# Down product of the third and fourth pair as seven block products for six of eight pieces, with the output projection last in the pair

## The reference

```python
# x: 8 chunks of 512 tokens, 512 features, float32
xn = layernorm(x)
q, k, v = xn @ Wq.T + bq, xn @ Wk.T + bk, xn @ Wv.T + bv
context = (elu(q) + 1) * cumsum((elu(k) + 1) * v, over tokens) * SCALE
s = context @ Wo.T + bo
h = fwht(xn * SU_ug) / 64                    # Walsh-Hadamard transform
u = silu(h @ W_gate.T * (Ws_gate * 64)) * (h @ W_up.T * (Ws_up * 64))   # 2048 wide
f = fwht(u * SU_dp) / 64 @ W_down.T * (Ws_down * 64)
out = x + s * silu(f)
```

## Time and profile before

| | |
|---|---|
| runs (3), us | median 1308.63, 1308.14 to 1309.26 |
| profiled execution, us | 1308.6 (the trace's span; no other run of it is shown) |
| granted TensorE clock | 0.998 of full |
| PE busy | 1276.1 us, 98%, 5968 matmuls |
| DVE busy | 886.8 us, 68% |
| ACT busy | 589.3 us, 45% |
| POOL busy | 59.1 us, 5% |
| DMA | 162 GB/s in the mean |

### The profile page before, as it was taken

One profiled execution on the slowest core, in us unless ns is written; L12 is line 12 of the kernel. 1 busy time (PEld: TensorE's weight loads), 2 busy tenths in 40 slices (PEclk: granted clock), 3 DMA queues, 4 the chain that ended last, 5 costly groups with the idle time before them and its releaser, 6 DMA issues.

```text
span 1308.6 us, 16031 instructions
## 1 busy us (share of the span) xinstructions
PE 1276.1 (98%) x5968; PEld 578.5 (44%) x5968; DVE 886.8 (68%) x1367; ACT 589.3 (45%) x880; POOL 59.1 (5%) x101
## 2 busy tenths in 40 slices
PE   5999999999999999999999999999999999999998
PEld 3544444444444444444444444444444444444443
DVE  6989999977756777777664755566762774555721
ACT  5875566631235655552324554442333654443220
POOL 1000101212000000110000000010000000000000
PEclk9999999999999999999999999999999999999999
DMA  9512552668764456653554323334453323323340
GB/s 374 212 65 89 174 188 113 216 243 286 207 251 149 145 207 239 206 185 129 193 193 161 129 97 129 112 147 161 161 195 129 126 99 127 119 107 112 114 156 37
DMA packets 56957, 212.03 MB, mean 162 GB/s; under 512 B 12208, under 2 KB 14512, under 8 KB 40368
## 3 DMA queue, kind: packets, MB, share of 16 engines
q1 hardware_dynamic: 45872, 179.55, 38.2%
q0 software_dynamic: 7536, 25.70, 5.8%
q10 hardware_dynamic: 3472, 5.77, 1.3%
HBM read 164.83 MB, written 46.16 MB: 161 GB/s over the span
## 4 chain that ended last, share of the span: by engine, by line
PE 58%; DVE 2%; issue 2%; ACT 2%; DMA 1%; DVEq 0%; ACTq 0%
PE bank L1875 39%; PE bank L1998 19%; DMA h_all<-scr_f 1%; DVE work L1261 1%; ACT work L922 1%; DVE work L1277 1%; ACT work L925 1%; DVE work L1267 0%; DVE h_all L1311 0%; DVE work L1302 0%; ACT work L905 0%; ACT L922 0%; DVE h_all L1424 0%; DVE h_all L1425 0%; DVE h_all L1601 0%
## 5 line engine op out<-in xcount | busy, mean ns | idle before, releaser
L1875 PE MATMUL bank<-xops,ring 128*128 128x512 f16 x2772 | 602.6, 379 | 8.6 <-DVE work L1261 3.3
L1875 PEld LDWEIGHTS bank<-xops,ring 128*128 128x128 f16 x2772 | 269.5, 98 | 340.6 <-issue 10.2
L1998 PE MATMUL bank<-h_all,ring 128*128 128x512 f16 x1536 | 333.8, 379 | 1.8 <-DMA ring<-scr_d 1.4
L1261 DVE TENSOR_TENSOR work<-bank,work 128x512 f32<-128x512 f32 x198 | 133.5, 686 | 163.2 <-PE bank L1875 150.5
L1998 PEld LDWEIGHTS bank<-h_all,ring 128*128 128x128 f16 x1536 | 149.9, 98 | 184.1 <-DVE work L1261 1.9
L1763 PE MATMUL bank<-xops,ring 128*128 128x512 f16 x1008 | 226.2, 381 | 2.5 <-DVE ring L1405 2.5
L905 ACT ACTIVATE work<-bank 128x512 f32<-128x512 f32 x198 | 117.8, 595 | 231.0 <-PE bank L1875 231.0
L1763 PEld LDWEIGHTS bank<-xops,ring 128*128 128x128 f16 x1008 | 98.4, 98 | 126.6 <-issue 10.5
L947 ACT ACTIVATE h_all<-work 128x512 f16<-128x512 f32 x128 | 78.1, 624 | 72.0 <-DVE work L1302 69.3
L1311 DVE TENSOR_TENSOR h_all<-work,h_all 128x512 f16<-128x512 f32 x128 | 87.4, 685 | 8.6 <-ACT h_all L947 7.5
L1267 DVE SCALAR_TENSOR_TENSOR work<-work 128x512 f32<-128x512 f32 x64 | 44.1, 689 | 49.7 <-ACT work L925 49.4
(11 more groups left out here) (210 smaller groups left out, 1023.0 us busy)
## 6 DMA issues: line engine op xcount, KB each, us to landing
ring<-scr_g SPq DMA_DIRECT2D x72, 1024.0 KB, 4.9
ring<-scr_d SPq DMA_DIRECT2D x32, 1024.0 KB, 5.4
scr_g<-ring SPq DMA_DIRECT2D x22, 512.0 KB, 3.3
h_all<-in_ug_t SPq DMA_DIRECT2D x8, 1024.0 KB, 12.3
x_res<-in_x_t SPq DMA_DIRECT2D x32, 256.0 KB, 4.3
out<-x_res SPq DMA_DIRECT2D x32, 256.0 KB, 4.4
scr_g<-ring POOLq DMA_DIRECT2D x12, 512.0 KB, 4.0
work<-in_x_t SPq DMA_DIRECT2D x6, 1024.0 KB, 7.3
```

The lines of the kernel that those rows point to most:

```text
L1261: dve.tensor_tensor(tile(g, j), at[:, :], tile(g, j), ALU.add).then_inc(summed, 1)
L1875: mm = pe.matmul(to[:, :], weight_of(slot, s, b, kk), at, start=(a == 0 and m in (P1, P2, P5)), stop=(a == 5), skip_group_check=True)
L1998: mm = pe.matmul(d_bank(c, t)[:, :], w[:, t, ws, :], at[:, s, :], start=(a == 0 and b == 0 and n == 0), stop=(a == KB - 1 and b == KB - 1 ...
```

## The change

Pairs 2 and 3 alone are changed in their products; what they need is prepared in pairs 0 and 1.

- The down product of both chunks of a pair is done at once. For pieces 0 to 5 it is seven block products of 18 matmuls, per output tile pair d = 0, 1 (`seven`); pieces 6 and 7 are added plainly (`rest`, 12 matmuls for each of four results and each d). That is 7 x 2 x 18 + 8 x 12 = 348 matmuls a pair, 384 before. It comes before the two Wo groups, which are now the last of the pair. The ring has four slots in these pairs.
- The operand sums of the hidden states are made as each up group ends: `hidden_sums` (four DVE operations of 128x512), `hidden_sums_high` (two on ACT), `hidden_sums_low` (two on DVE), in place of one high and one low operation.
- The S sums of the down weights are made in six units u = 0 to 5. ACT's queue stores the float32 down weights to memory (`df_stored`); POOL loads a unit (4 DMAs of 128 KB) and stores it (2 DMAs); DVE adds (`unit_add`, four operations of 128x256) and makes the low part (`unit_low`); ACT makes the high part (`unit_high`). Units 0 to 3 lie in the last chunk of pair 1, units 4 and 5 at the ends of groups 0 and 1 of pair 2.
- The down weights get one common scale, so squares of all four tiles are taken first: tiles 2 and 3 are loaded as a probe, 0 and 1 after them, then 2 and 3 again. The levels of the Hadamard butterfly on the down weights (`fly_down_level`) come one tile later in the order of the first groups, and the scale is worked out once, not four times.
- The statistics of pair 3 are taken in groups 8 and 10.
- Outputs of a pair are made together (`pair_outputs`): four around the Wo groups, four in groups 0 and 1 of the next pair (two each), and for the last pair after everything else.

```diff
+SEVEN_FROM, SEVEN = 2, 6
+REST = FP - SEVEN
+REST_BANKS = (6, 7)
+R11, R21, R22, R12 = range(7, 11)
+DOWN_SLOTS = (P1, P2, P6, P7, P5, R11, P4, P3)
+DOWN_ORDER = [(d, m) for ms in ((P1, P2), (P6,), (P7,), (P5,), (R11,), (R21,), (R22,), (R12,), (P4,), (P3,))
+              for d in range(2) for m in ms]
+DOWN_COPIES = ((0, P1), (1, P1), (0, P6), (1, P6), (0, P7), (1, P7))
+DOWN_SUMS = [(d, a) for a in ("22a", "11", "22", "12") for d in range(2)]
...
+PROBE, SQUARE_DOWN_AT = (2, 3, 0, 1), (15, 16, 19, 20)
...
-FLY_DOWN_AT, SCALE_DOWN_AT = (0, 1, 2, 3), 4
+FLY_DOWN_AT, SCALE_DOWN_AT = (1, 2, 3, 4), 4
...
+STATS_AT, LATER_STATS_AT = (16, 18), (8, 10)
...
+            load_probe(2)
+            load_probe(3)
...
                     store_piece(n)
+                if n == QKV_GROUPS - 1:
+                    load_down(0)
+                    load_down(1)
...
+            def load_unit(u):
+
+                d, q = u % 2, u // 2
+                if u < 2:
+                    pool.wait_ge(quad_done, 3 * KB)
+                    pool.wait_ge(df_stored, 16 * KB)
+                else:
+                    pool.wait_ge(unit_summed, u - 1)
+                for r in range(2):
+                    src = scr_df[d + 2 * r, :, :].rearrange("p (c k n) -> p c k n", c=2, k=FP)
+                    for half in range(2):
+                        pool.dma_start(unit_raw(u)[:, half, :, r, :], src[:, half, 2 * q:2 * q + 2, :]) \
+                            .then_inc(unit_loaded[u % 2], 16)
+
+            def store_unit(u):
+                d, q = u % 2, u // 2
+                pool.wait_ge(unit_made, u + 1)
+                to = scr_s[:, :, d, 512 * q:512 * q + 512].rearrange("o p n -> p o n")
+                for a in range(2):
+                    pool.dma_start(to[:, 2 * a:2 * a + 2, :],
+                                   unit_part(u, 2)[:, a, :].rearrange("p (o n) -> p o n", o=2)).then_inc(unit_stored[u % 2], 16)
...
+                if p == SEVEN_FROM - 1:
+                    load_unit(0)
+                    load_unit(1)
+                    for u in range(UNITS):
+                        store_unit(u)
+                        if u + 2 < UNITS:
...
+            def unit_high(u):
+                act.wait_ge(unit_summed, u + 1)
+                if u >= 2:
+                    act.wait_ge(unit_stored[u % 2], 32 * (u // 2))
+                act.activation(unit_out(u)[:, :, :, HI, :], unit_sums(u).rearrange("p c (m n) -> p c m n", m=4),
+                               ACT.Copy).then_inc(unit_hi, 1)
...
+            def hidden_sums_high(p, i):
+
+                g = QKV_GROUPS + 2 * i + 1
+                act.wait_ge(hidden_summed, sums_of_hidden(p, i))
+                act.activation(h[:, i, TILE_OF[C12], HI, :], tile(g, C12), ACT.Copy).then_inc(h_hi, 1)
...
+                three = work[:, 4 * (g % 3):4 * (g % 3) + 3, :]
+                act.activation(home(i)[:, :, HI, :], three, ACT.Copy).then_inc(hidden_sums_hi, 1)
...
                 if g:
                     take(p, g - 1, C12)
                 take(p, g, C11)
+                if p == SEVEN_FROM and g < UNITS - 4:
+                    unit_high(4 + g)
...
+            def seven_and_o(p):
+
+                seven_copy(p, 0, P1)
+                seven_copy(p, 1, P1)
+                seven_copy(p, 0, P6)
+                ctx_high(p, 0)
+                seven_copy(p, 1, P6)
+                seven_copy(p, 0, P7)
+                seven_copy(p, 1, P7)
+                ctx_high(p, 1)
+                if p < PAIRS - 1:
+                    x_high(p + 1, 0)
+                    t_high(p + 1, 0)
+                    x_high(p + 1, 1)
+                    t_high(p + 1, 1)
+                for d, j in GATE_ORDER:
+                    seven_gate(p, d, j)
+                o_groups(p)
...
-                if p < PAIRS - 1:
-                    x_high(p + 1, 0)
-                    t_high(p + 1, 0)
-                    x_high(p + 1, 1)
-                    t_high(p + 1, 1)
+                x_high(p + 1, 0)
+                t_high(p + 1, 0)
+                unit_high(0)
+                x_high(p + 1, 1)
+                unit_high(1)
...
+            def hidden_sums(p, i, part):
+
+                g = QKV_GROUPS + 2 * i + 1
+                b11, b22, b21, b12 = (tile(g, j) for j in (C11, C22, C21, C12))
+                if part == 0:
+                    dve.wait_ge(h_made, 32 * p + 4 * i + 4)
+                    prep.after(dve.tensor_tensor(b12, b12, b11, ALU.subtract))
+                    prep.after(dve.tensor_tensor(b22, b22, b12, ALU.subtract))
+                else:
+                    dve.tensor_tensor(b11, b22, b11, ALU.subtract)
+                    dve.tensor_tensor(b21, b21, b22, ALU.subtract).then_inc(hidden_summed, 1)
...
+            def hidden_sums_low(p, i):
+                g = QKV_GROUPS + 2 * i + 1
+                at = h[:, i, TILE_OF[C12], :, :]
+                dve.wait_ge(h_hi, 32 * p + 4 * i + 4)
+                dve.tensor_tensor(at[:, LO, :], tile(g, C12), at[:, HI, :], ALU.subtract).then_inc(h_ready, 1)
+                three = work[:, 4 * (g % 3):4 * (g % 3) + 3, :]
+                dve.wait_ge(hidden_sums_hi, sums_of_hidden(p, i))
+                dve.tensor_tensor(home(i)[:, :, LO, :], three, home(i)[:, :, HI, :], ALU.subtract) \
+                    .then_inc(hidden_sums_ready, 1)
...
+            def pair_outputs(p, ns):
+                for n in ns:
+                    d, j = OUT_ORDER[n]
+                    gated(2 * p + CHUNK_OF[j], d + 2 * ROW_OF[j])
...
+            def unit_add(u):
+
+                a11, a12, a21, a22 = (unit_raw(u)[:, half, :, r, :] for r in range(2) for half in range(2))
+                dve.wait_ge(unit_loaded[u % 2], 64 * (u // 2 + 1))
+                if u >= 2:
+                    dve.wait_ge(unit_made, u - 1)
+                prep.after(dve.tensor_tensor(unit_sum(u, S1), a21, a22, ALU.add))
+                dve.tensor_tensor(unit_sum(u, S3), a11, a21, ALU.subtract)
+                prep.after(dve.tensor_tensor(unit_sum(u, S2), unit_sum(u, S1), a11, ALU.subtract))
+                dve.tensor_tensor(unit_sum(u, S4), a12, unit_sum(u, S2), ALU.subtract).then_inc(unit_summed, 1)
...
+            def unit_low(u):
+                dve.wait_ge(unit_hi, u + 1)
+                to = unit_out(u)
+                dve.tensor_tensor(to[:, :, :, LO, :], unit_sums(u).rearrange("p c (m n) -> p c m n", m=4),
...
                 use(p, g, C11)
+                if p > SEVEN_FROM and g < 2:
+                    pair_outputs(p - 1, (4 + 2 * g, 5 + 2 * g))
+                if p == SEVEN_FROM and g < UNITS - 4:
+                    unit_add(4 + g)
+                    unit_low(3 + g)
+                    if g == UNITS - 5:
+                        unit_low(4 + g)
                 if p == 1 and late_sums(g - 1) is not None:
...
+                    t_low(p + 1, 1)
+                for d, a in DOWN_SUMS[2:]:
+                    seven_add(p, d, a)
+                for j in (C11, C22, C12):
+                    add(p, GROUPS, j)
+                pair_outputs(p, (0, 1))
+                add(p, GROUPS + 1, C11)
+                add(p, GROUPS + 1, C22)
+                pair_outputs(p, (2, 3))
...
-                    x_sums(p + 1, 1)
-                    t_low(p + 1, 1)
+                x_sums(p + 1, 0)
+                t_low(p + 1, 0)
+                unit_add(0)
+                x_sums(p + 1, 1)
+                unit_add(1)
+                unit_low(0)
+                t_low(p + 1, 1)
+                unit_add(2)
+                unit_low(1)
+                unit_add(3)
+                unit_low(2)
                 outputs(2 * p + 1)
+            pair_outputs(PAIRS - 1, range(4, 8))
...
+                    product(p, g, P3)
+                    for d, m in DOWN_ORDER[1:]:
+                        if m < R11:
+                            seven(p, d, m)
+                        else:
+                            rest(p, d, m)
                 elif g + 1 == GROUPS:
                     down_part(2 * p, 0, (0, 1))
...
+                to = {R11: right_bank(d), R21: chain_bank(d), R22: bank[REST_BANKS[d]], R12: left_bank(d)}[m]
+                terms = [(i, half, s, xs) for i in range(SEVEN, FP) for half in range(2)
...
                         first_group(g)
                     else:
                         group(p, g)
-                for a in range(KB):
-                    if a or not p:
-                        down_quad(2 * p, a)
```

More of the change, by code:

```diff
@@ L79 @@
 C11, C22, C21, C12 = range(4)
+GATE_ORDER = [(d, j) for j in (C11, C22, C21, C12) for d in range(2)]
+OUT_ORDER = [(d, j) for d in range(2) for j in (C11, C22, C21, C12)]
 PLAIN_BANKS = (0, 1, 2, 3)
@@ L305, in build @@
         o_stored = sem("o_stored")
+        df_stored = sem("df_stored")
+        unit_loaded = [sem(f"unit_loaded{u}") for u in range(2)]
+        unit_stored = [sem(f"unit_stored{u}") for u in range(2)]
+        res_loaded = [sem(f"res_loaded{c}") for c in range(2)]
```

(41 more changed lines are left out.)

426 lines of the change are left out of this document (334 added, 92 removed).

## The result

The changed kernel took 1317.08 us in the median of 5 runs (1316.54 to 1323.87), the kernel before 1308.84 (5 runs): ratio 1.0075, 95% interval 1.0055 to 1.0095. It is slower, by some 8 us, where 1314.3 had been predicted. In a second set of runs it took 1316.07 against 1309.38, ratio 1.0054 (1.0041 to 1.0067).

The account below looks back on a forecast made before the run. PE, busy 1276.1 of 1308.6 us, was taken to bound the kernel. Savings of 15.6 in matmuls and 1 in pair 0, against added waits, clock loss and tail, summed to +5.7: 1314.3 us, range 1306 to 1320.

Parts of the forecast that it names:

- Matmuls: Down products of the third and fourth pairs: 72 fewer matmuls at 0.216 us each, -15.6 us.
- rival of 131 ns a matmul: All removed matmuls: worth only 9.4 us, not 15.6, so a time of about 1320 us; chance 0.01.
- Preparation in pair 0: First pair: butterfly levels moved later and scale worked out once, against extra loads and earlier squares, -1 us.
- Units 2 and 3: End of the second pair: their loads and sums delay ACT's silus and copy in the next group 0, +3.0 us.
- Unit 5: Part 5, third pair's group 1: its sum and low parts stand before DVE's times v, +4.1 us.
- Clock: PE's clock falls behind waits at the starts of the third pair, +2.4 us, and fourth pair, +1.7 us.
- Steady groups: Third pair's up groups: added hidden-sum work brings DVE to about 75% busy and costs nothing, 0 us.
- End of the third pair: P5's slot load behind the means' reload, and a DVE add 0.8 late for R12: +0.9 us.
- Tail: After PE's last matmul: a Wo add and four outputs make 8.7 us of 4.8, +3.9 us.
- loads in the way: SP's queue stalls behind the probe's second load or the means, a slot 4 to 8 late: 1318 to 1322; chance 0.07.
- no change: Third pair's start: clock stays up and units come in time, 1307 to 1311 us; chance 0.18.
- rival in which the insertions are hidden: Units 4 and 5 and two outputs fall into DVE's and ACT's idle time: 1299.8 us; chance 0.14.

Follow-up runs that it names:

- again: The changed kernel with no edit, run a second time for another execution's rows: 1316.07 us, ratio 1.0054 to the kernel before.
- the first execution: The profiled execution in the first set of runs of the changed kernel, no edit: 1323.87 us.
- units45_idle: Changed kernel with units 4 and 5 of the S sums moved out of the third pair's groups 0 and 1: 1308.86 us, ratio 0.9996.
- ring_rotated: Changed kernel with the four-slot ring beginning at slots 3 and 4, not 1 and 2: 1317.10 us, ratio 1.0060.
- best_rotated: Changed kernel with units 3 to 5 moved later, outputs in DVE's idle times, P5's load earlier, ring beginning at slots 3 and 4: 1297.39 us, ratio 0.9909.

## Why the prediction was right, point by point

- *Matmuls, -15.6.* Right: the two down stages fell by 7.6 and 8.1. The rival of 131 ns a matmul is refuted: 36 of them would have been worth 4.7 a stage. Here the Trainium skill's "TensorE: Matmul & The Clock Gate", section "Back-to-back issue gap", with about 131 ns for a sustained matmul of 512 columns, and the trace, with 216, differ, and the trace decides.
- *Preparation in pair 0, -1.* -0.4 in again, +0.1 at the same milestone in the first execution (107.97 for 107.84). The wait of 2.51 shrank to 0.4 as I had it, but the levels moved along came out as new waits at the next three places (0.84, 0.83 and 1.66 us). The size can't be told: in the ten other traces of changed kernels, again among them, the third pair began at 695.9 to 698.3, in the kernel before at 697.67.
- *Units 2 and 3, +3.0.* 1.68 + 0.75 = 2.4. The path was right, the sizes a little off: in again the units' 24 loads landed 2.8 to 8.5 us after their issue, median 3.4, where I took 3.1. By the fit in the Trainium skill's "DMA: Bandwidth & Descriptors", section "Anatomy of one DMA — SWDGE (gpsimd) path", an estimate for 128 KB is 2.3, below every one of them. What I missed is that a second wait, for the ring, lay under this one; it would have made the rival "units come in time" worth only part of its 3 us.
- *Unit 4, +3.6.* 3.63 for ACT's copy (3.68 in again), less the 0.23 that were there: +3.4.
- *Unit 5, +4.1.* 2.01 + 1.88 - 0.20 = 3.7, in two waits, not in one: one for ACT (`unit_high(5)` ahead of the copy), which I hadn't priced, and the rest for times v.
- *Clock, +2.4 and +1.7.* In the third pair of again 42 matmuls took 11.78 us, 2.6 more than the 9.22 of units45_idle. That near hit is luck: I had given the wait of part 5 no clock cost of its own, and in five of the seven executions that have these waits it had one. In the first execution 42 took 10.93 and 66 took 16.69, 1.7 and 2.3 more, 4.0 in all, so there the term is 1.6 too small. In the fourth pair 66 took 16.09, 1.7 more than 14.40, as forecast. What I had taken for a rule is a chance (last section).
- *Steady groups, 0.* Right: PE was busy 50.00 of 50 us in the window from 800 to 850 in again, though DVE had 40.51 us of it, against 25.59 before: 81%, not 75%. The cover is thinner than I said.
- *End of the third pair, +0.9.* The wait for P5's slot was 2.02 in one execution, 0.32 in ring_rotated, and at most 0.2 in again and the six others with this order of loads. A chance, not a constant. The late add for R12, 0.8 in my sum, made PE wait 0.24 in again.
- *Fourth pair, +2.7.* 2.66, by the row.
- *Tail, +3.9.* 4.6: I left out that outputs 2 and 3 still held DVE when the last product ended, 0.76 us.

The mechanism was right in all the large terms, and the sum is within 0.3 us of again's difference of spans. That close is in part luck: stage by stage the errors are +0.6, -0.5, -0.7, -0.1, -0.3 and +0.7 us and cancel, and again is one of the two executions in which only one run of the third pair's matmuls was slow. The 1.8 us between 1314.3 and again's 1316.07 are a step of another kind: I set the sum against the span, 1308.6, and said that it equals the median. It doesn't. In each execution a run's time is 1.8 us above its span (1315.86 for 1314.0; of before 1309.21 for 1307.4), and the profiled execution of before was about 1 us longer than the usual one (1309.38 less 1.8 is 1307.6). From medians the change is +6.7 to +8.2, so the sum of +5.7 was 1.0 to 2.5 us short.

The rival "loads in the way" came true in part, in one execution: 3.02 us for down weights in pair 0, behind the reload of the means as the rival has it, and 2.02 for P5's slot, which stands behind such a reload too. The rival "no change" needed units in time and the clock up; in no execution of the changed kernel were both so. The rival in which the insertions are hidden was false for the kernel as changed, and true for the work as such: moved by a few places in the queues the same operations cost 0.3 us in the third pair of best_rotated and nothing in the fourth.

## What to carry over

In this kernel DVE work was free in steady groups, even with DVE 81% busy, and cost nearly its full length at a pair's start, where PE waits for DVE's and ACT's next operation. So look for the idle time that follows the last operation another engine is waiting for, and put the work there, but check that its own input has landed by then. When a wait is taken away, the next one under it comes out (here a ring whose restart put an early load into the last slot to be freed), so price a repair by what is late next, and test it with the cover gone: the same line was worth 0 with the cover and 3.2 us without. For small terms trust the row at the place, not the median.
